# Two bulk loads of a graph-gather kernel cut into 1 KB pieces in place of one piece per partition

## What is computed

```python
mask = A != 0                                            # A: [8, 2048, 2048] int32
scores = jnp.where(mask, -arange(N), -inf)
vals, idx = jax.lax.top_k(scores, 25)                    # the 25 neighbours of lowest number
feats = where(vals > -inf, X[idx], -inf)                 # their feature rows
agg = feats.max(axis=2)
agg = where(degree <= 25, maximum(agg, 0.0), agg)
out = relu(concat([X, agg], -1) @ W + b)                 # W: [512, 256]
return layernorm(X + out)
```

## Time and profile before

| | |
|---|---|
| median of 3 runs | 2715.47 us (2704.24 to 2724.01) |
| the profiled execution | 2719.33 us, its span 2717.6 us |
| busy share of the span | PE 81%, DVE 82%, ACT 70%, POOL 70% |
| DMA, hardware queue of SP (q1) | 199.20 MB, 20.8% of the 16 engines' span |
| DMA, software queue of POOL (q0) | 114.59 MB, 16.5% of the 16 engines' span |

### The profile page before, as it was taken

How to read it: one execution, slowest core, us unless ns; L and a number is a source line. 1 busy time by engine, 2 the same in 40 slices (tenths; PEclk the granted TensorE clock), 3 DMA queues, 4 the chain that set the end, 5 groups by cost and what they waited for, 6 DMA issues and landing times.

```text
span 2717.6 us, 45794 instructions
## 1 busy us (share of the span) xinstructions
PE 2188.4 (81%) x12707; PEld 1697.6 (62%) x12832; DVE 2235.2 (82%) x4807; ACT 1909.3 (70%) x3314; POOL 1913.4 (70%) x1861
## 2 busy tenths in 40 slices
PE   4887588848885788888887888848887888888885
PEld 2666466636664666667665666637665766667674
DVE  2888689958885988989877888959887888888896
ACT  7777478737774687877776777837777777677762
POOL 3776777777675776677767777777776777776775
PEclk9999799979997899999998999979999999999998
DMA  5333434343345232433343333443334333343321
GB/s 190 127 110 116 76 126 155 118 93 102 120 141 114 86 125 95 162 119 123 113 138 119 115 119 106 153 103 114 118 105 149 114 111 125 98 134 118 113 61 48
DMA packets 143746, 317.31 MB, mean 117 GB/s; under 512 B 53438, under 2 KB 79434, under 8 KB 126018
## 3 DMA queue, kind: packets, MB, share of 16 engines
q1 hardware_dynamic: 61250, 199.20, 20.8%
q0 software_dynamic: 82176, 114.59, 16.5%
HBM read 405.28 MB, written 16.78 MB: 155 GB/s over the span
## 4 chain that ended last, share of the span: by engine, by line
DMA 44%; issue 25%; POOL 14%; PE 6%; DVE 6%; ACT 4%; POOLq 1%; DVEq 0%; ACTq 0%
DMA got<-in_x,index 44%; POOL got L430 12%; PE near_ps L699 3%; DVE nearest L815 2%; PE out_ps L719 2%; POOL got_more L425 2%; ACT mask_t L515 1%; PE out_ps L655 1%; ACT val L510 1%; POOLq L438 1%; DVE hot L801 0%; ACT squares L558 0%; POOLq L456 0%; DVE got L924 0%; DVE first_far L859 0%
## 5 line engine op out<-in xcount | busy, mean ns | idle before, releaser
L430 POOL DMA_INDIRECT got<-in_x,index x1664 | 1857.2, 1116 | 755.0 <-issue 447.5
L699 PE MATMUL near_ps<-heads,hot 128*128 128x256 f32 x5920 | 1411.3, 390 | 272.1 <-DVE nearest L815 269.1
L699 PEld LDWEIGHTS near_ps<-heads,hot 128*128 128x128 f32 x5920 | 1143.6, 196 | 523.6 <-DVE nearest L815 320.2
L815 DVE TENSOR_TENSOR nearest<-near_ps,nearest 128x1024 f32<-128x1024 f32 (+2 forms) x632 | 748.7, 1185 | 141.6 <-PE near_ps L699 116.4
L546 ACT ACTIVATE got<-ones_col 128x3328 f32<-128x3328 f32 x128 | 382.4, 2987 | 0.0
L510 ACT ACTIVATE val<-z_ps,rank_col 128x1024 f16<-128x1024 f32 (+1 forms) x256 | 226.5, 885 | 158.9 <-PE z_ps L666 158.5
L475 ACT ACTIVATE flag<-out_ps 1x1 int32<-1x1 f32 x128 | 20.5, 160 | 404.4 <-PE out_ps L655 399.1
L801 DVE TENSOR_SCALAR hot<-val 127x128 f32<-127x128 f16 (+7 forms) x896 | 282.2, 387 | 0.0
L529 ACT ACTIVATE far<-val,beyond 128x128 bf16<-128x128 f16 (+7 forms) x488 | 253.6, 589 | 0.1
L515 ACT ACTIVATE mask_t<-adj_sb 128x2048 bf16<-128x2048 int32 x128 | 242.9, 1897 | 0.0
L519 ACT ACTIVATE mask_t<-mask_t 128x2048 bf16<-128x2048 bf16 x128 | 242.4, 1894 | 0.0
(11 more groups left out here) (124 smaller groups left out, 2319.1 us busy)
## 6 DMA issues: line engine op xcount, KB each, us to landing
adj_sb<-in_adj_turned SPq DMA_DIRECT2D x128, 1024.0 KB, 4.9
xx_sb<-in_x_both SPq DMA_DIRECT2D x128, 256.0 KB
got<-in_x,index POOLq DMA_INDIRECT x1664
out<-y SPq DMA_DIRECT2D x128, 128.0 KB
heads<-in_x_near SPq DMA_DIRECT2D x8, 1536.0 KB, 8.6
hot<-vacant SPq DMA_DIRECT2D x80, 12.0 KB
got_more<-in_x,index_more POOLq DMA_INDIRECT x48, 8.0
w_sb<-in_L_gnn_W SPq DMA_DIRECT2D x1, 512.0 KB, 12.1
```

What stands on the lines that cost most here:

```text
L430: pool.indirect_dma_start(out=to, out_offset=None, in_=x_rows, in_offset=bass.IndirectOffsetOnAxis(ap=at, axis=0), bounds_check=a.g * (N + ...
L699: mm = pe.matmul(near_ps[:, buffer_of(a, k), s - k * ROUND:s - k * ROUND + 1, :], hot[:, a.i, s * P:(s + 1) * P], heads[:, a.side, c, None ...
L815: dve.tensor_tensor(nearest[:, a.i, 0:n, :], near_ps[:, buffer_of(a, k), 0:n, :], nearest[:, a.i, 0:n, :], ALU.max).then_inc(near_taken, 1)
```

## The change

Both calls get an argument that caps the contiguous piece moved by one descriptor, here at 1024 bytes. It applies to every load of an adjacency strip (128 of them, through `load_adj`), and to the six loads of `heads` inside the steps; the loads of `heads` for the first two graphs are not touched.

```diff
+ROW_PIECE = 1024
...
             def load_adj(a):
-                sp.dma_start(adj_sb[:, a.i, :], adj_turned[a.T]).then_inc(adj_in[a.i], 16)
+                sp.dma_start(adj_sb[:, a.i, :], adj_turned[a.T], max_dma_last_dim=ROW_PIECE).then_inc(adj_in[a.i], 16)
...
-                    sp.dma_start(heads[:, a.side, :, :], x_near[a.g + 2]).then_inc(heads_in[a.side], 16)
+                    sp.dma_start(heads[:, a.side, :, :], x_near[a.g + 2], max_dma_last_dim=ROW_PIECE).then_inc(heads_in[a.side], 16)
```

## The result

The changed kernel takes 2747.47 us (median of 7 runs, 2733.87 to 2753.50) against 2710.61 us of the kernel before (7 runs). The ratio of the means, 2743.90 to 2711.75 us, is 1.0119, with a 95% interval of 1.0085 to 1.0152: slower by 1.2%, where 2.2% faster was forecast; the medians alone would give 1.4%. The profiled execution took 2735.61 us, its span 2733.9 us: it is one of the faster ones of the changed kernel, 16.3 us longer than the profiled execution before.

What follows compares the result with a forecast made beforehand. POOL, waiting for its own gathers, was taken to bound the kernel. Of 125 us removed from POOL's waits, DVE's room allowed 67, 60 taken: 2715.5 - 60 = 2655 us, likeliest range 2633 to 2680, wider range 2630 to 2746.

Steps and rivals of the forecast that it cites:

- The bound: POOL waits for its own gathers into `got`; about 177 us of real waiting, mostly where an adjacency strip blocks them.
- The slack of 5.2 us: Time a gather may take to land before POOL notices: four in flight at 1.30 us each.
- The step that failed: Strip's 64 pieces per DMA engine taken in slowly, so gathers land in 3.5 us; 125 us of POOL's waiting removed.
- a turn of some 9 to 17 descriptors: DMA engines alternate between queues; a turn shrinks from 2.46 us to 0.7 us, with the same gain; no separate chance.
- First come, first served: On each DMA engine, a strip's 8 pieces, taken in within about half a microsecond, run before gathers issued later.
- The slower rival: Strip's 64 pieces per engine go in at once, holding gathers 0.26 us longer; 31 us, 2746 us in all; chance 0.20.
- DVE's room: DVE's waits for gathers before L924 and L911 cap the gain at 67 us; 60 taken.
- What was taken for nothing: SP's issue of 1024 pieces, 0.69 us estimated, and slower 1 KB moves of strips (0.26 us each) and heads cost nothing.

## Why the prediction was wrong

**The bound was read rightly.** POOL, its four gathers in flight and the strip that blocks them once per tile set the end. Eight in flight, eight transfers and two halves apart each lessen the stall by another road, and each is faster by 0.9 to 1.6%. Counted in each trace over the 1511 to 1596 gathers whose 16 marks could all be told, the share that took more than 5.2 us to land goes with the time: 15.6% in the changed kernel (ratio 1.012), 15.0% with two transfers at once (1.003), 14.0% with 2 KB pieces (1.002), 12.7% before, 11.8% with four transfers (0.995), 7.1% with eight (0.986), 5.5% with two halves apart (0.984).

**The slack of 5.2 us** came out right in part by luck. POOL's next gather starts 0.80 us after a landing that it had to wait for (median of 159 waits before, 161 after), 0.50 more than the prediction allowed; but a gather costs 1.12 + 0.30 us on the mean, more than the 1.30 that it took. That makes 4 x 1.42 - 0.80 = 4.9 us, and in the trace of before the gaps begin where a gather takes 5.0 to 5.5 us. For the same reason the gather of 1010.11 did not take until about 1016.5: its last mark is at 1016.06.

**The step that failed** is this one: "If 8 pieces are taken in over half a microsecond, 64 need about 4 us at the same pace". The half microsecond came from the wrong gather of the earlier trace rows, as shown above, and it was put down to pieces, while it belongs to the transfer. With 64 pieces per engine the limit for a gather moves by 0.3 us at most and not to 4 us, and behind it 592 packets ran ahead of the gather, 37 per engine. So no short queue of pieces stands ahead of a gather, but the whole strip.

The Trainium skill ("DMA: Bandwidth & Descriptors", "Queues, rings and completion order") names a turn of some 9 to 17 descriptors with a ceiling of 64, and the prediction leaned on the 9 to 17 for support; with 37 per engine in the same view this trace does not show them, and the measurement decides. A strip of 64 pieces per engine would just fill a turn at the ceiling, so the strips alone leave that rival standing. The heads, 96 pieces per engine, speak against it: SP's issue of a load of heads in the changed kernel, a gather 1.08 us behind it in the chain, and the DMA from 416.7 to 420.9 us.

```profile
415.34 0.39 SPq L340 DMA_DIRECT2D heads<-in_x_near  x1
```

```profile
416.42 7.67 DMA got<-in_x,index
```

```profile
q1 hardware_dynamic: 1290, 1.31, 94.0%
q0 software_dynamic: 4, 0.00, 0.1%
```

1290 packets, some 80 per engine, ran with four of POOL's among them. POOL's issue of that gather ended at 417.41; had SP's queue given way after its first 64 pieces on each engine, the gather would have got in before the end of this stretch.

**First come, first served** fits all of this: a gather that is handed over early enough gets in, one behind the strip waits. How an engine chooses between queues was not seen directly. The prediction's sentence on the gather of 1010.11 ("The trace agrees: the gather issued at 1010.11, before the strip, landed only behind it") reads too much into it. That gather's issue ended 0.88 us behind SP's, and its data ran only from 1014.66 on; the marks from 1010.9 to 1011.4 are those of the gather before it. So it shows the wait for the strip, and nothing on the order in which marks land.

**The slower rival was right in mechanism, and near in price.** It said that the pieces go in all at once and the block grows by 0.26 us, 31 us in all and 2746 us. The means differ by 32 us and the medians by 37; that 2746 meets the median of 2747.5 so closely is luck, as the kernel before stood at 2715.5 in three runs and at 2710.6 in seven. In the profiled executions POOL's wait grew by 38 us, 0.32 us per strip, 0.06 more than the rate of the packets gives. A strip of small pieces also starts more slowly: from 1.0 to 2.0 us behind SP's issue the first strip shown of each kernel moved, before and after,

```profile
q1 hardware_dynamic: 20, 0.16, 87.8%
```

```profile
q1 hardware_dynamic: 106, 0.11, 45.0%
```

which is 0.05 MB less, 0.13 us at 385 GB/s. Why a strip lands 0.9 us later, more than rate and start explain, and why a gather behind it takes only 0.2 us longer, was not settled. The error in the judgement was to give this rival 0.20 and the forecast 0.56, on an estimate for a queue of 64 pieces of which no row existed.

**DVE's room** was put at 67 us, 60 of it to be had. Where POOL's stall goes, 0.984 x 2711 = 2668 us is reached, 43 us. The cap was right in kind (POOL waits 126.5 us for DVE with eight in flight) but a third too large: DVE's waits for gathers were counted as free, while a part of them turns into waits for PE's products. These were 116.4 us before and are 135.4 us with the two halves apart and 147.0 us with eight transfers. The upper bound of the range, 2680, is the profiled execution less 40 us; from the median it would have been some 2675.

**What was taken for nothing**: the heads cost nothing that the run can tell (1.0004, 0.9980 to 1.0028), SP's issue of a strip takes 0.40 us, between the 0.34 of before and the estimate of 0.69, and 1 KB pieces cost nothing by themselves once the blocks are short (0.9840 beside 0.9842).

## What to carry to other kernels

When a bulk load holds up small indirect transfers on the same DMA engines, cutting its descriptors did not let them in here; cut the transfer itself and issue its parts at different times, so that no part is longer than the small transfers' slack. Work out that slack first, here about 5 us for four gathers in flight: a delay below it cost POOL nothing, and above it POOL paid once per tile. When packets of two queues run together, find out by the completion marks whose packets they are before a rule is built on them. Before pricing a gain, look at what is bound next: the two halves took 86 of POOL's 177 us of waiting away, and that was worth 43 us.

## What the runs showed of the hardware

One transfer of 1024 descriptors is handed over to the DMA engines nearly as fast as one of 128: in either kernel a gather whose issue ended 0.8 to 1.0 us behind SP's waited for the whole strip (6.13 and 5.92 us to land, 2.7 us where no strip is near). Smaller pieces in one transfer did not let the other queue in, not even after some 80 packets per engine. POOL's next gather starts 0.80 us after a landing that it had to wait for. A transfer to 16 neighbouring partitions is much slower than one to 16 spread partitions: with the same eight transfers of 8 KB pieces per strip, an 8 KB packet took 820 ns on the mean in the one and 477 in the other, SP's queue took 38.0% of the DMA engines' span and 26.7%, and the kernel 2977 us against 2680.
